# An early-fusion kernel: the setup's stores and fetches split over two queues, products on a zero tile beside its own products, and statistics of row pairs with a shared residual step in the feed-forward loop

## What is computed

```
x: (64, 64, 75, 3) frames of 75 joints; txt: (64, 32, 64)
for layer in 0, 1, 2:   x = A @ (x @ W) + b; x = (x - m) * g * rsqrt(v + eps) + be; relu in 0 and 1
h = concat(mean over the joints, txt)                    # (64, 96, 64)
h = h + attention(layernorm(h))
f = layernorm(h)
30 times: f = f + 0.01 * tanh(f)
          f = f * sigmoid(f)
          f = layernorm(f, ln_w, ln_b);  f = f @ W.T + b
out = h + f
```

## Time and profile before

| | us |
|---|---|
| median of 3 runs | 1889.93 (1888.03 to 1891.75) |
| the profiled execution's own time | 1891.53 |
| its span, first to last instruction | 1889.7 |
| PE / DVE / ACT / POOL busy | 1803.5 / 1518.0 / 1239.2 / 834.8 |
| first product of `tokenise` | at 80.74 |
| first `bn_stats` of `feed_forward` | at 1428.66 |

### The profile page before, as it was taken

The page is one execution under the profiler, slowest core; times in us unless marked ns, Lnnn a source line. Parts: engine busy times, 40 slices in busy tenths (PEclk is TensorE's granted clock), DMA queues, the critical chain, the costliest instruction groups (busy, mean ns, idle before and its releaser), DMA issues. The chain is left out here.

```text
span 1889.7 us, 76961 instructions
## 1 busy us (share of the span) xinstructions
PE 1803.5 (95%) x25670; PEld 1551.5 (82%) x25701; DVE 1518.0 (80%) x4601; ACT 1239.2 (66%) x2918; POOL 834.8 (44%) x850
## 2 busy tenths in 40 slices
PE   8399999999999999999999999999597999999998
PEld 7299999999999999999999999999493777777776
DVE  5488888888888888888888888888568888888887
ACT  1377777777777777777777777777153666666665
POOL 1033322333223332333223332233056999999997
PEclk9999999999999999999999999999787999999999
DMA  4200000000000000000000000000210000000000
GB/s 95 82 9 8 8 8 8 8 8 8 8 8 8 8 8 8 8 8 8 8 8 8 8 8 8 8 8 7 61 46 22 0 0 0 0 0 0 0 0 34
DMA packets 50049, 25.51 MB, mean 13 GB/s; under 512 B 24553, under 2 KB 47988, under 8 KB 49652
## 3 DMA queue, kind: packets, MB, share of 16 engines
q1 hardware_dynamic: 47831, 24.26, 5.9%
q10 hardware_dynamic: 1972, 0.86, 0.2%
q0 software_dynamic: 224, 0.11, 0.0%
HBM read 16.23 MB, written 8.93 MB: 13 GB/s over the span
## 5 line engine op out<-in xcount | busy, mean ns | idle before, releaser
L654 POOL TENSOR_TENSOR y0lo<-y_whole,y0hi 125x384 f16<-125x384 f32 x410 | 376.1, 917 | 905.4 <-ACT y_whole L612 905.4
L616 ACT ACTIVATE z1hi<-ps 128x375 f16<-128x375 f32 x820 | 397.7, 485 | 343.8 <-PE ps L555 343.8
L679 DVE TENSOR_TENSOR z1lo<-ps,z1hi 128x375 f16<-128x375 f32 x820 | 449.7, 548 | 194.8 <-ACT z1hi L616 194.8
L554 PE MATMUL ps<-ATlo,y0hi 125*128 125x150 f16 x2460 | 585.7, 238 | 0.0
L553 PE MATMUL ps<-AThi,y0hi 125*128 125x150 f16 x2460 | 567.9, 242 | 3.3 <-POOL y0lo L654 3.3
L555 PE MATMUL ps<-AThi,y0lo 125*128 125x150 f16 x2460 | 565.5, 239 | 0.0
L684 DVE TENSOR_TENSOR y<-ps,negb 125x384 f32<-125x384 f32 x820 | 450.8, 550 | 29.7 <-PE ps L570 0.7
L568 PE MATMUL ps<-W1hi,z1hi 128*128 128x128 f16 x2460 | 459.4, 221 | 0.2 <-DVE y L684 0.2
L570 PE MATMUL ps<-W1hi,z1lo 128*128 128x128 f16 x2460 | 453.9, 219 | 0.0
L569 PE MATMUL ps<-W1lo,z1hi 128*128 128x128 f16 x2460 | 453.6, 219 | 0.0
L608 ACT ACTIVATE y0hi<-ps 125x384 f16<-125x384 f32 x820 | 405.8, 495 | 21.4 <-PE ps L533 21.4
(11 more groups left out here) (196 smaller groups left out, 2343.1 us busy)
## 6 DMA issues: line engine op xcount, KB each, us to landing
z_static<-z_rows SPq DMA_DIRECT2D x1640, 4.4 KB
pooled_rows<-stage SPq DMA_DIRECT2D x820, 2.5 KB
xs<-in_x_v SPq DMA_DIRECT2D x5, 720.7 KB, 12.5
z_rows<-zp SPq DMA_DIRECT2D x15, 234.4 KB
parts<-pooled_rows SPq DMA_DIRECT2D x8, 256.0 KB, 6.3
h_rows<-h SPq DMA_DIRECT2D x16, 96.0 KB, 1.8
h2r<-h_rows SPq DMA_DIRECT2D x6, 256.0 KB, 2.6
out<-h2r SPq DMA_DIRECT2D x6, 256.0 KB, 2.1
```

The costliest lines, as they stand in the source:

```text
L554: nc.tensor.matmul(o, hi, alo, start=False, stop=False, skip_group_check=True)
L616: nc.scalar.activation(z1hi[:, q, 0:GV], ps[:, Z1B + q % 2, 0:GV], ACT.Identity).then_inc(z1hi_done, 1)
L654: nc.gpsimd.tensor_tensor(y0lo[0:R, par, q, :], y0f[0:R, q, :], y0hi[0:R, par, q, :], ALU.subtract).then_inc(y0lo_by_pool, 1)
L679: nc.vector.tensor_tensor(z1lo[:, q, 0:GV], ps[:, Z1B + q % 2, 0:GV], z1hi[:, q, 0:GV], ALU.subtract).then_inc(z1lo_done, 1)
```

## The change

**Setup.** The PSUM banks of the products become six; the seventh (`BANKS`) keeps its small products and the eighth (`SPARE`) takes 512-column products of a zero tile, which nothing reads: 16 ahead of the first product, one behind each, 24 at the end. SP holds back loads 2 to 4 of `xs` until the parameters have landed. ScalarE computes the first high part after 12 products, not after 20. The small products move forward between the large ones. Of the four stores of a slab SP keeps two and GpSimd takes two; SP fetches iterations 0 and 1 behind the stores of slab 0, in the setup.

**Tokenise.** A fetch is four DMAs of 12 rows (a source row read twice) for eight of 6 rows.

**Feed-forward.** One `bn_stats` reads two rows of 64 in turn, element by element, so its even and odd halves are the two rows' statistics: four of 128 elements for eight of 64. `dm`, `s`, `q` and GpSimd's sum go; one `tensor_scalar` makes `var`. The residual product stays on PE for even chunks and becomes one VectorE operation on PSUM for odd ones. `gn` and the transposes come one step earlier.

```diff
+def fetch(eng, zs, zst, zst_loaded, it, par):
+    src = zs[:, :, :, bass.ds(it, 1)].rearrange("q w c one e -> q (w c) (one e)")
+    for q in range(QUART):
+        eng.dma_start(zst[32 * q:32 * q + 4 * CIN, par, 0:GV],
+                      src[q].rearrange("(one r) e -> one r e", one=1).to_broadcast([2, 2 * CIN, GV])).then_inc(zst_loaded[par], 16)
...
-        BANKS = 7
+        busy = sb("busy", [P, 512], F16)
+        BANKS = 6
+        SPARE = 7
...
+            def store_z(eng, stored, k, firsts, rest):
+                f0, even, units = k * ZF, ZF - 1, slice(k * QUART, (k + 1) * QUART)
+                eng.wait_ge(zhi_done, k + 1)
+                eng.wait_ge(zlo_done, k + 1)
+                for c in firsts:
+                    eng.dma_start(zs[:, :, c, f0:f0 + even].rearrange("q w f e -> f q w e"),
+                                  zp[c * ZF:c * ZF + even, units]).then_inc(stored, 16)
+                if rest:
+                    eng.dma_start(zs[:, :, :, f0 + even].rearrange("q w c e -> c q w e"),
+                                  zp[even:ZP:ZF, units]).then_inc(stored, 16)
...
+                    if k == 2:
+                        sp.wait_ge(loaded, NPAR * 16)
                     sp.dma_start(xs[:, k, :], x_v[:, k]).then_inc(x_loaded[k], 16)
+                sp.wait_ge(zst_clear, 1)
                 for k in range(ZK):
...
+                    store_z(sp, z_stored[k][0], k, (0, 1), False)
+                    if k < 2:
+                        for stored in z_stored[0]:
+                            sp.wait_ge(stored, ZSTORES * 16)
+                        fetch(sp, zs, zst, zst_loaded, k, k)
...
-                for n in range(ZN):
-                    z_whole(n)
-                act.wait_ge(zf_done, ZN)
-                act.wait_ge(sz_ready, 1)
...
+                for n in range(2, 3 * QUART):
+                    z_whole(n)
+                act.wait_ge(sz_ready, 1)
                 z_high(0)
...
-                for k in range(2, ZK):
+                z_high(2)
+                for k in range(3, ZK):
+                    for n in range(k * QUART, (k + 1) * QUART):
+                        z_whole(n)
                     z_high(k)
...
+                def keep_busy(n):
+                    for i in range(n):
+                        nc.tensor.matmul(ps[:, SPARE, :], busy[:, 0:P], busy[:], start=True, stop=True)
...
+                    keep_busy(1)
...
+                    if n == 11:
+                        pe.wait_ge(cvec_ready, 1)
...
+                    if n == 15:
+                        pe.wait_ge(stack_ready, 5)
+                        pe.wait_ge(id_made, 2)
+                        nc.tensor.transpose(ps[:, BANKS, C:2 * C], stack[:], ident[:]).then_inc(stack_t, 1)
+                keep_busy(24)
...
+                    for j in range(CP):
+                        last = v_.bn_stats(pairs[:, b, j, :], src[:, 2 * j:2 * j + 2, :].rearrange("p i d -> p d i"))
+                    last.then_inc(bns, 1)
                     dve.wait_ge(bns, n + 1)
...
+                    v_.tensor_scalar(var[:, b, :], squares(pairs, b), D * EPS, None, ALU.add).then_inc(made, 1)
...
+                    if on(0) and c % 2 == 1:
+                        dve.wait_ge(th_done, s + 1)
+                        v_.scalar_tensor_tensor(ps[:, c, :], th[:, c % 2, :], 0.01, ps[:, c, :],
+                                                ALU.mult, ALU.add).then_inc(y_ready[1], 1)
```

More of the change, by code:

```diff
@@ L160, in setup @@
         band_clear = sem("band_clear")
+        busy_clear = sem("busy_clear")
+        zst_clear = sem("z_static_clear")
         at_loaded = sem("at_loaded")
@@ L418, in _, with tokenise @@
                     mix_input(n)
[L419 to L428, removed]
+                    keep_busy(1)
+                    if n == 3:
+                        pe.wait_ge(pool_filled, 1)
+                        pe.wait_ge(abar_ready, 1)
+                        nc.tensor.matmul(ps[:, BANKS, 0:1], ones[0:V, :], acol[:, 1:2], start=True, stop=True).then_inc(asum_ready, 1)
+                    if n == 11:
+                        pe.wait_ge(cvec_ready, 1)
+                        nc.tensor.matmul(ps[:, BANKS, D:2 * D], cvec[:], w2[:], start=True, stop=True).then_inc(const_ready, 1)
+                    if n == 15:
[3 more added lines that the diff above has]
+                keep_busy(24)
+def tokenise(nc, ps, zs, zst, z_stored, zst_loaded, pooled_dram, AThi, ATlo, abar, W0K, W1hi, W1lo, negb1):
     with ExitStack() as ctx:
@@ L487, in _ @@
             def _(sp):
[L488 to L492, removed]
                 def store(it, par):
@@ L498, in store @@
                         sp.dma_start(pooled_rows(it)[q], stage[32 * q:32 * q + GF, par]).then_inc(stored[par], 16)
[L500 to L505, removed]
+                for pair in z_stored[1:]:
+                    for stored_k in pair:
+                        sp.wait_ge(stored_k, ZSTORES * 16)
                 def body(it, par, pair, last=False):
@@ L510, in body @@
                         sp.wait_ge(y0_ready, it + 1)
-                        fetch(it + 2, par)
+                        fetch(sp, zs, zst, zst_loaded, it + 2, par)
                     if late(it, 2):
@@ L1263, in _, with body @@
                 nc.scalar.activation(warm[:], ident[:, 0:1], ACT.Silu)
-                def body(s, c, on):
+                def body(s, c, on, half):
                     if on(0):
@@ L1302, in body @@
                         last.then_inc(x_ready, 1)
-                    if on(4):
-                        n, b = s - 4, c % 2
+                    if on(0) and c % 2 == 0:
+                        pe.wait_ge(th_done, s + 1)
+                        nc.tensor.matmul(ps[:, c, :], pct[:], th[:, c % 2, :], start=False, stop=True,
+                                         skip_group_check=True).then_inc(y_ready[0], 1)
+                    if on(3):
+                        n, b = s - 3, (c - 3) % 2
                         pe.wait_ge(gn_done, n + 1)
@@ L1330, in centre @@
                 def centre(c):
                     b = c % 2
+                    rows = h2[:, c, :].rearrange("p (r d) -> p r d", d=D)
                     dve.wait_ge(h2_loaded, (c + 1) * 16)
                     if c >= 2:
-                        dve.wait_ge(var0_done, c - 1)
-                    for r in range(CR):
-                        last = v_.bn_stats(bs0[:, b, r, :], h2[:, c, r * D:(r + 1) * D])
-                    last.then_inc(bn0, 1)
-                    statistics(bs0, dm0, s20, q20, b, c, diff0, parts0_done, bn0)
@@ L1346, in first @@
+                        dve.wait_ge(centred, c - 1)
+                    statistics(rows, bs0, var0, b, c, bn0, var0_done)
+                    v_.tensor_tensor(x0c[:, b, :].rearrange("p (r d) -> p r d", d=D), rows,
+                                     spread(means(bs0, b), P, CR), ALU.subtract).then_inc(centred, 1)
                 def first(c):
@@ L1364, in body @@
                                          spread(rs[:, b, :], P, CR), ALU.mult).then_inc(gn_done, 1)
[L1365 to L1366 removed]
+                    if on(1):
+                        n, cn, b = s - 1, (c - 1) % CH, (c - 1) % 2
                         dve.wait_ge(g_done, n + 1)
                         if late(n, 2):
[L1369 to L1377 removed]
+                            dve.wait_ge(rs_done, n - 1)
+                        statistics(g_[:, cn % NG], bs, var, b, n, bn_done, var_done)
                 steps(dve, body, first)
```

144 lines of the change are left out of this document (54 added, 90 removed).

## The result

The changed kernel takes 1814.3 us (median of 4 runs, 1812.4 to 1816.6) where the kernel before takes 1890.7 (1888.0 to 1891.8): 0.9598 of its time, 95% interval 0.9582 to 0.9615, 76 us less. The profiled execution has a span of 1813.5 us, 76.2 less than before.

A forecast was written before the change was run, and what follows sets the result against it. It took TensorE's chain and an equally tight VectorE-GpSimd ring to bound the feed-forward, plus the setup ahead of the tokeniser. -53.5 (loop) - 4 - 20.5 (setup) - 2 = -80 from 1891.53: 1811.5, some 1809 at the median; range 1787 to 1842.

The forecast's parts named there:

- With one input I take half, 0.3 ns: Feed-forward statistics: the strided read costs 0.3 ns an element, 0.038 us more each, 1.12 us for the four.
- the ring: Feed-forward loop: power on GpSimd, then `gn` and statistics on VectorE, back to power; 1.97 to 2.24 us a step after.
- the second rival: Feed-forward loop: no stride cost, few powers inside a `gn`; TensorE sets 1.98 a step, -74 us, 1788; 10%.
- the last steps: End of the feed-forward: with transposes two chunks ahead a step is 1.55 us; 5 x 0.86, -4 us.
- The residual operation stands ahead of `gn` in its step, but it waits only for a tanh that ScalarE has made: Feed-forward, VectorE: the moved residual, 0.30 us a step, falls into the time in which the power runs.
- taking work off TensorE alone would therefore bring nothing: Feed-forward: a chain through VectorE and GpSimd is as tight as TensorE's 2.41 us a step; both must shorten.
- The block ends at 59.7: End of the setup, behind stores and 24 zero products; the tokeniser's first product follows at 60.2, -20.5 us.
- The tokeniser's first product: Tokeniser start, used as the mark of the setup's gain: at 60.2 for 80.74, -20.5 us.
- the -2 for a warm start: Tokeniser start: its first matmuls, 6.1 us at half rate before, start at the high clock level; -2 us, at most -3.
- The fourth rival: Setup: TensorE stays at 1.2 GHz throughout, the end near 69; -11 us for -22.5, 1820; 12%.
- The first steps ... I take 0: Feed-forward's first steps, at the 1.2 GHz level: lost small operations against a later clock rise; 0, 4 us either way.
- The third rival: Feed-forward loop: `gn` waits for a power that has begun; 2.42 us a step, no gain in the loop, 1863; 6%.

The follow-up runs named there:

- the kernel meant for it: Changed setup with the feed-forward of before, only the residual of odd chunks moved to VectorE ahead of `gn`: 1958.4 us, 1.0376 of the kernel before.
- the early subtraction: Changed kernel plus a one-column GpSimd subtraction in the setup, behind the all-reduce and ahead of GpSimd's stores: 1806.3 us, 0.9565 of the kernel before.
- the kernel meant for that: Combined version (subtraction, earlier x0 work, reordered stores) with more zero products and the subtraction ahead of the all-reduce: 1805.8 us, 0.9553 of the kernel before.

## Why the prediction came out as it did

**The loop: right mechanism, a term too large.** I took 2.10 a step; it is 2.00. The step that failed is "With one input I take half, 0.3 ns": the strided read costs nothing. The four statistics take 0.92 for 1.12, so VectorE needs 1.92 for 2.12, and the ring comes out at its lower end, where TensorE's 0.22 + 0.89 + 0.44 + 0.43 sets the pace. That is the second rival (1.98, 10%). The loop and the last steps give 72.3 for 57.5; the last steps are as foretold (bias products 1.54, 1.60, 2.22, 1.60, 1.10 apart, 8.1 for five against 12.05).

**"The residual operation stands ahead of `gn` in its step, but it waits only for a tanh that ScalarE has made"**: true as it was built, by luck, since the reason isn't in the prediction. It holds by the step order; with the order of before it costs 212 us. I read the chain and the ring through GpSimd, and not the ring that the moved operation closes. That "taking work off TensorE alone would therefore bring nothing" is not shown either way: the kernel meant for it closed this ring, and none has the old statistics with the new step order.

**The setup: a mis-sized end.** Up to there my figures hold: `sz` at 34.8 for 34.7, the last product done at 50.4 for 50.7. "The block ends at 59.7" fails: I let zero products and stores end it, and never asked when GpSimd's queue is empty. Its drain ends at 62.7 (+3.0). The kernel that took the last stores from it shows that this sets the end.

**The tokeniser's start: a cost that was hidden.** "The tokeniser's first product" was the wrong mark; the first mix is what counts. Before, GpSimd's `y0lo` started at 83.57, 7.5 us behind its `MODIFY_POOL_CONFIG` at the block's start, and SyncE's fetch covered nearly all of that (the first mix 3.8 us behind the first product, for 2.5 with the early subtraction). I cut the fetch and not this: the first mix comes 9.2 us behind the first product instead of 3.8. The Trainium skill (GPSIMD Engine Reference, Instruction dispatch) states a cost of this kind: the first call to newly loaded code pays about 6 us, with no instruction of its own shown in the profile, counted from the `MODIFY_POOL_CONFIG`. The trace agrees in kind and gives 6.9 to 8.2; that the all-reduce is what makes the arithmetic's code be loaded anew fits the rows and is not shown. Drain and late arithmetic, 3 + 5.4, are the whole miss of the setup (20.5 - 12.3 = 8.2), and the -2 for a warm start is nothing.

**The zero products** are no reason for any of the gain. The fourth rival (level low in the setup) had the level right from 19.9 on and the price wrong: it took 2.55 a product with its zero product, and without zero products 12 are done by 33.2, in time at 1.2 GHz too.

**"The first steps ... I take 0"** failed: +9.7. I counted the work that each step loses and not the order on VectorE, where the statistics of s-1 now stand ahead of x0's next chunk.

**The third rival** (`gn` waits for a running power) falls, at `gn` 1646.39. The Trainium skill (SBUF — State Buffer, SBUF: two separate sides) states that whichever of the two starts first blocks the other. The trace differs where GpSimd is first: a running power doesn't hold up a `gn` with two SBUF inputs.

**The sum** has a slip of 1: 1811.5 less 1.6 is 1810, not 1809.

Open: whether TensorE held at 2.4 GHz from the setup into the first mixes would bring anything. In the kernel meant for that the zero products ended the block, and TensorE stood idle for 7.7 us behind them.

## What to carry to other kernels

When an operation moves to another engine, follow its result all the way round to its own next input, and count steps of slack: the same work in the same place cost 212 us or nothing by one step of order. When a load or fetch is shortened, look at what else began at the same instant and was hidden behind it. A queue's end is when it has drained, not when it has issued.

## What the hardware showed beyond that

- GpSimd's first arithmetic behind an all-reduce starts 6.9 to 8.2 us behind a `MODIFY_POOL_CONFIG` in its queue, once, with its inputs ready.
- GpSimd's drain at the end of a block lasts until 6.5 us behind its last issued store (56.2 to 62.7), 4.9 to 7.6 over all kernels here; SyncE's takes 0.2 to 0.5.
- Statistics over two interleaved rows, every element 256 bytes from the last, take 282 ns for 128 elements against 211 for 64 in line: 1.1 ns an element, as in line.
